# Narrow attention: two heads per stacked operand, on partitions 0 and 64, without padding

## The chip, the cores and the metric

The kernel runs on one core of one Trainium2 chip. The metric is the device time of one launch in microseconds. Before the change, three runs took 3659.43, 3660.25 and 3673.93 us; their median is 3660.25 us.

## The reference, cut to what matters

The whole program is a network of sixteen layers on an activation of 4 batch rows x 512 tokens x 128 features. Two of the sixteen are a "narrow" multi-head attention with 16 heads of 8 features each. The layers L0b and L2b compute, for each batch row,

```
q = (LN(x) Wq^T + bq) * scale      k = LN(x) Wk^T + bk      v = LN(x) Wv^T + bv
s[h] = q[h] k[h]^T                 (512 x 512 for each of 16 heads; L2b only for keys <= query)
out  = concat_h( softmax(s[h]) v[h] ) Wo^T + bo + x
```

Scale is 19.5/128 in L0b and 8^-0.5 in L2b. The other fourteen layers are not touched.

## The kernel before, in words

The activation lies transposed, features on partitions. A hardware loop runs twice, each time over two batch rows (`NB = 2`), through all sixteen layers, so each narrow attention is executed four times in all: L0b twice, L2b twice. In the profile its tiles carry the names `L0b_...` and `L2b_...`. Every engine has its own program, written out by hand (`block.sync` for the transfers, `block.tensor`, `block.scalar`, `block.gpsimd`, `block.vector`), and the engines meet only at semaphores. Nothing is scheduled by a planner: each engine takes its instructions strictly in the order of the code.

The products of q and k are made in bf16, at nearly the precision of float32. VectorE cuts q and k into three bf16 parts (`cut`, lines 1389 to 1397); the six products of parts that matter are put below each other, 8 features x 6 = 48 rows of the contraction (`Q_PART`, `K_PART`, `ROWS`). The rows are rearranged by way of a buffer in memory, `parts_dram`: `send_parts` (line 1225) writes all parts of a batch row in one transfer, and `stack` (line 1233) reads them back in twelve transfers for one **unit**. A unit is four heads of one batch row; there are `UN = 8`. Each head has a slice `qs[:, b, i, r, :]` of all 128 partitions; rows 48 to 50 of q take three bf16 parts of minus the row's maximum, against ones in k, and GpSimd has filled the other rows with zeros (q) and ones (k).

For each unit TensorE first makes all scores once with queries on the partitions (`top_scores`, line 1278, 16 of them: 4 heads x 4 blocks of 128 queries), VectorE takes the largest of each row (line 1403), the 17th step turns the 16 columns of maxima (line 1273), VectorE negates and cuts them (lines 1411 to 1421), and three small transfers put them into rows 48 to 50 of `qs` (line 1246). Then TensorE makes the scores a second time with keys on the partitions (`scores`, line 1294), with the maximum already subtracted, ScalarE takes the exponential (line 1356), and TensorE multiplies by v (`products`, line 1309), four heads side by side in 32 columns each. The v operand `vpad` carries ones in eight further columns, so the denominators come out of the same product. L2b adds a mask matmul (lines 1281 and 1297) behind each score matmul.

The order is by **slots**: 64 slots of two heads x 128 keys each. In slot s TensorE issues `scores(s)`, in even slots `products(s/2-1)`, and then two or three `top_scores` of a later unit. Before the first slot, `LEAD = 25` steps of the maxima are made. The maxima go through two PSUM banks, so TensorE can be at most two steps ahead of VectorE. After each 16 slots a finished group of eight heads is normalised: ScalarE copies the sums out, one float32 matmul spreads the denominators (line 1316), and VectorE takes the reciprocal of 128x512, multiplies and adds the bias (lines 1427 to 1431). At the end come the output projections (line 1335).

SyncE issues all transfers. Its order is: parts of batch row 0, stacks of units 0 and 1, parts of batch row 1, and then for each unit u its maxima and the stack of unit u+2.

Of the kernel before, what the change touches and what calls it, by code (L numbers as in the profile page):

```python
# [1161 lines left out]
Q_PART = (0, 0, 1, 1, 0, 2)  # L1162
K_PART = (0, 1, 0, 1, 2, 0)
# [3 lines left out]
def narrow_attention(g, name, w, causal, scale):  # L1167

    STACK = 16 * 2 * len(Q_PART)
    AHEAD = 2
    LEAD = 25
    UN = NB * 4
    with Stage(g, name) as st:  # L1180
# [12 lines left out]
        mcut = st.sb("mcut", [16, 2, 3, P], BF16)  # L1193
        inv = g.xn[:, 0, :]
        def acc(c):
            return (ln.xc, ln.sq)[c // 2][:, c % 2, :]

        proj, proj_in, cuts, cuts_act, stacked, ones_in, v_in, zero, vpad_ready = (
            st.sem(n) for n in ("proj", "proj_in", "cuts", "cuts_act", "stacked", "ones_in", "v_in", "zero", "vpad_ready"))
        top, top_in, m_steps, m_rows = (st.sem(n) for n in ("top", "top_in", "m_steps", "m_rows"))  # L1200
        score, prob, pv, inv_ready, at_ready, at_bias, out_ready, added = (
            st.sem(n) for n in ("score", "prob", "pv", "inv_ready", "at_ready", "at_bias", "out_ready", "added"))
        parted, ones_put, copied, spread = (st.sem(n) for n in ("parted", "ones_put", "copied", "spread"))
        mask_qk, mask_kq = g.cb[:, P:2 * P], g.cb[:, 2 * P:3 * P]
# [13 lines left out]
        with g.nc.Block() as block:  # L1218
            @block.sync
            def _(sp):  # L1220
                st.clear_spent(sp)

                def send_parts(b):
                    sp.wait_ge(cuts, 5 * b + 5)
                    sp.dma_start(g.parts_dram[b], cut[:, :, :, :]).then_inc(parted, 16)
                    sp.wait_ge(parted, 16 * (b + 1))

                def stack(u):
                    b, i = u // 4, u % 4
                    for j in range(len(Q_PART)):  # L1230
                        for x, part, dst in ((0, Q_PART[j], qs), (1, K_PART[j], ks)):
                            src = g.parts_dram[b, :, part, x, :].rearrange("(r i f) t -> i f r t", r=4, i=4)[i]
                            sp.dma_start(dst[DH * j:DH * j + DH, b, i, :, :], src).then_inc(stacked, 16)
                    sp.wait_ge(stacked, STACK * (u + 1))

                send_parts(0)
                sp.wait_ge(ones_in, 2)
                for u in range(AHEAD):
                    stack(u)
                send_parts(1)  # L1240
                sp.wait_ge(ones_in, 2 * NB)
                for u in range(UN):
                    b, i = u // 4, u % 4
                    sp.wait_ge(m_steps, 6 * u + 6)
                    for p in range(3):
                        sp.dma_start(qs[ROWS + p:ROWS + p + 1, b, i, :, :].rearrange("o r (t c) -> o (r t) c", c=P),
                                     mcut[:, u % 2, p, :]).then_inc(m_rows, 16)
                    sp.wait_ge(m_rows, 48 * (u + 1))
                    if u + AHEAD < UN:
                        stack(u + AHEAD)  # L1250

            @block.tensor
            def _(pe):
                ln.tensor(pe)
                for b in range(NB):
                    pe.wait_ge(ln.done, NB)
                    if b >= 1:
                        pe.wait_ge(proj_in, 2 * b)
                        pe.wait_ge(v_in, b)
                    pe.matmul(g.ps[:, 0, :], g.w(w + "_wq"), g.xn[:, b, :], start=True, stop=True)  # L1260
                    pe.matmul(g.ps[:, 1, :], g.w(w + "_wk"), g.xn[:, b, :], start=True, stop=True)
                    for t in range(KT):
                        mm = pe.matmul(g.ps[:, 2, t * P:(t + 1) * P], g.xn[:, b, t * P:(t + 1) * P], g.w(w + "_wv"), start=True, stop=True)
                    mm.then_inc(proj, 1)

                def top_scores(u, n):
# [8 lines left out]
                    if n == 0:  # L1275
                        pe.wait_ge(stacked, STACK * (u + 1))
                    r, t = n // 4, n % 4
                    mm = pe.matmul(g.ps[:, 4 + a % 2, 0:span(t)], qs[:, b, i, r, t * P:(t + 1) * P], ks[:, b, i, r, 0:span(t)],  # L1278
                                   start=True, stop=not causal)
# [4 lines left out]
                def scores(s):  # L1284

                    u, kt, half = s // 8, s // 2 % 4, s % 2
                    b, i, q0 = u // 4, u % 4, first(s // 2 % 4)
                    if kt == 0 and half == 0:
                        pe.wait_ge(m_rows, 48 * (u + 1))
                    if s >= 2:  # L1290
                        pe.wait_ge(prob, s - 1)
                    for x in range(2):
                        r, bank = 2 * half + x, 2 * (s % 2) + x
                        mm = pe.matmul(g.ps[:, bank, q0:T], ks[:, b, i, r, kt * P:(kt + 1) * P], qs[:, b, i, r, q0:T],  # L1294
                                       start=True, stop=not causal)
                        if causal:
                            mm = pe.matmul(g.ps[:, bank, q0:q0 + P], eye, mask_kq, start=False, stop=True)  # L1297
                    mm.then_inc(score, 1)

                def products(n):  # L1300

                    b, i, kt, q0 = n // 16, n // 4 % 4, n % 4, first(n % 4)
# [3 lines left out]
                    if n % 8 == 0 and b >= 1:  # L1306
                        pe.wait_ge(inv_ready, n // 8 - 1)
                    for r in range(4):
                        mm = pe.matmul(g.ps[32 * r:32 * r + 32, 6 + i // 2, q0:T], vpad[:, b, kt, 4 * r + i, :], pt[:, n % 3, r, q0:T],
                                       start=(n % 8 == 0), stop=(n % 8 == 7), skip_group_check=True)  # L1310
                    mm.then_inc(pv, 1)

                def spread_den(c):

                    pe.wait_ge(copied, c + 1)
                    pe.matmul(g.ps[:, 6 + c % 2, :], g.w("den_of"), acc(c), start=True, stop=True).then_inc(spread, 1)

                pe.wait_ge(ones_in, 2 * NB)
                pe.wait_ge(v_in, NB)
                for a in range(LEAD):  # L1320
                    top_scores(a // 17, a % 17)
                for s in range(8 * UN):
# [5 lines left out]
                    if s % 16 == 4 and s > 16:  # L1328
                        spread_den(s // 16 - 1)
                products(4 * UN - 1)  # L1330
                spread_den(2 * NB - 1)
                for b in range(NB):
                    pe.wait_ge(at_bias, 2 * b + 2)
                    for c in range(2):
                        mm = pe.matmul(g.ps[:, b, :], g.w(w + "_wo", c * P, P), acc(2 * b + c), start=(c == 0), stop=(c == 1))
                    mm.then_inc(out_ready, 1)

            @block.scalar
            def _(act):
                ln.scalar(act)  # L1340
                for b in range(NB):
                    act.wait_ge(proj, b + 1)
                    act.activation(v[:, b, :, :], g.ps[:, 2, :].rearrange("p (t c) -> p t c", c=P), ACT.Copy).then_inc(v_in, 1)
# [880 lines left out]
```

## Time and profile before

| | us |
|---|---|
| median of three runs | 3660.25 |
| the profiled execution, whole | 3659.59 |
| its span, first to last instruction | 3657.6 |
| granted TensorE clock over the span | 0.887 of full speed |
| one execution of L0b (271.7 to 469.9) | 198.2 |
| one execution of L2b (1170.0 to 1343.0) | 173.0 |

In the page's sums TensorE is busy for 75% of the span, VectorE 52%, ScalarE 40%, GpSimd 15%. These are averages over sixteen different layers. All times below are positions in the span of the profiled execution; what is said of a layer is read inside its own stretch. "PE" is TensorE's matmuls, "PEld" its weight loads, "DVE" VectorE, "ACT" ScalarE, "POOL" GpSimd, "SPq" transfers issued by SyncE. A float32 matmul shows as two PE instructions in the counts.

### The profile page before, as it was taken

To read this page: it belongs to the slowest core of one execution; us is meant where nothing else is said; L and a number is where in the kernel's file an instruction comes from. 1 tells how busy PE (TensorE), PEld (TensorE's weight loads), DVE (VectorE), ACT (ScalarE), POOL (GpSimd) and SP (SyncE) were. 2 spreads that over 40 slices of the span, in tenths; PEclk is the share of its full clock that TensorE was granted. 3 is DMA by queue.
4 is the path that set the end of the run, shared out by engine and by line. 5 is a ranking of instruction groups with operands and counts; after the bars stand their busy time and mean duration, and the time that the engine had idled before them with its cause. 6 is when DMAs were issued, how large, how long until landed. Compare 5 with 4: busy or idle time off the path is not lost. (4 is left out here: it accounts for less than half of the span.)

```text
span 3657.6 us, 33867 instructions
## 1 busy us (share of the span) xinstructions
PE 2741.8 (75%) x12082; PEld 1218.6 (33%) x12082; DVE 1890.3 (52%) x2639; ACT 1451.8 (40%) x2368; POOL 558.9 (15%) x324
## 2 busy tenths in 40 slices
PE   3565769899878579466746657789997877894677
PEld 1221145445344234123212211554443433341232
DVE  4867642455122751595649586415552237416955
ACT  2442511555234244343524424125552433443434
POOL 0533000000003101161006320000000040011600
PEclk8897977999989799799968979689999898997999
DMA  2001000000010210000000020000000102100000
GB/s 91 0 1 39 15 0 1 1 1 1 0 46 1 44 50 6 0 1 1 1 13 0 0 43 11 1 1 1 1 1 0 46 9 41 51 0 0 0 1 6
DMA packets 31504, 48.18 MB, mean 13 GB/s; under 512 B 7520, under 2 KB 19808, under 8 KB 31328
## 3 DMA queue, kind: packets, MB, share of 16 engines
q1 hardware_dynamic: 31328, 45.93, 4.8%
q8 instruction: 98, 1.61, 0.2%
q14 instruction: 78, 0.64, 0.1%
HBM read 38.18 MB, written 7.34 MB: 12 GB/s over the span
## 5 line engine op out<-in xcount | busy, mean ns | idle before, releaser
L1598 ACT ACTIVATE L1b_pr<-ps,L1b_mneg 128x512 f32<-128x512 f32 x256 | 173.8, 684 | 195.7 <-DVE L1b_mneg L1637 195.7
L518 POOL TENSOR_TENSOR xs<-xs,L2f_part 128x512 f32<-128x512 f32 x32 | 40.5, 1264 | 1287.6 <-DVE L2f_part L507 1287.6
L1356 ACT ACTIVATE L0b_pt<-ps 128x1024 f32<-128x1024 f32 x128 | 129.6, 1024 | 209.4 <-PE ps L1294 209.4
L1635 DVE TENSOR_REDUCE L1b_m<-ps 128x2 f32<-128x1024 f32 x128 | 156.7, 1224 | 105.0 <-PE ps L1502 101.0
L90 ACT ACT_TABLE_LOAD x34 | 43.6, 1283 | 419.6 <-PEq L671 181.4
L1403 DVE TENSOR_REDUCE L0b_mx<-ps 128x1 f32<-128x512 f32 x256 | 161.2, 684 | 47.7 <-PE ps L1278 45.0
L1046 POOL TENSOR_TENSOR L0a_db<-L0a_du,L0a_bs 128x1024 f32<-128x1024 f32 x64 | 150.3, 2353 | 227.8 <-ACT L0a_bs L1017 217.1
L1046 POOL TENSOR_TENSOR L3a_db<-L3a_du,L3a_bs 128x1024 f32<-128x1024 f32 x64 | 150.3, 2353 | 226.5 <-ACT L3a_bs L1017 216.0
L1356 ACT ACTIVATE L2b_pt<-ps 128x1024 f32<-128x1024 f32 (+3 forms) x128 | 88.4, 704 | 204.2 <-PE ps L1297 203.7
L1278 PE MATMUL ps<-L0b_ks,L0b_qs 128*128 128x512 bf16 x256 | 104.0, 446 | 87.0 <-DMA L0b_ks<-parts_dram 51.8
L1661 DVE COPY L1b_prt<-ps 128x512 f32<-128x512 f32 x128 | 88.5, 691 | 125.0 <-PE ps L1513 124.7
L1122 DVE TENSOR_TENSOR_SCAN L0a_hs<-ps,L0a_db 128x1024 f32<-128x1024 f32 x64 | 146.1, 2283 | 9.9 <-ACT ps L1009 8.0
L1122 DVE TENSOR_TENSOR_SCAN L3a_hs<-ps,L3a_db 128x1024 f32<-128x1024 f32 x64 | 146.1, 2282 | 9.8 <-ACT ps L1009 8.0
L1403 DVE TENSOR_REDUCE L2b_mx<-ps 128x1 f32<-128x128 f32 (+3 forms) x256 | 116.7, 486 | 54.0 <-PE ps L1281 52.4
L1502 PE MATMUL ps<-L1b_k,L1b_q 64*128 64x512 f32 x512 | 144.0, 640 | 0.0
L1525 PE MATMUL ps<-L1b_prt,L1b_v 128*64 128x512 f32 x512 | 136.7, 614 | 4.1 <-issue 2.0
L1513 PE MATMUL ps<-weights,L1b_pr 128*128 128x128 f32 x1024 | 135.8, 275 | 3.0 <-ACT L1b_pr L1598 3.0
L1278 PE MATMUL ps<-L2b_ks,L2b_qs 128*128 128x128 bf16 (+3 forms) x256 | 80.1, 347 | 76.5 <-DMA L2b_ks<-parts_dram 50.2
L1513 PEld LDWEIGHTS ps<-weights,L1b_pr 128*128 128x128 f32 x1024 | 115.6, 141 | 50.6 <-issue 43.5
L507 DVE SCALAR_TENSOR_TENSOR L2f_part<-ps,weights,L2f_masks 128x512 f32<-128x512 f32 x32 | 24.0, 751 | 205.7 <-PE ps L439 205.7
L946 PE MATMUL ps<-L0a_hc,weights 128*128 128x512 f32 x256 | 127.7, 623 | 2.7 <-DVE L0a_hc L1127 2.7
L507 DVE SCALAR_TENSOR_TENSOR L2g_part<-ps,weights,L2g_masks 128x512 f32<-128x512 f32 x32 | 24.0, 751 | 203.7 <-PE ps L439 203.7
(564 smaller groups left out, 5853.1 us busy)
## 6 DMA issues: line engine op xcount, KB each, us to landing
L2f_w<-expert_dram SPq DMA_DIRECT2D x32, 256.0 KB, 3.0
L2g_w<-expert_dram SPq DMA_DIRECT2D x32, 256.0 KB, 3.0
weights<-w_dram SPq DMA_DIRECT2D x7, 820.5 KB, 9.3
parts_dram<-L0b_cut SPq DMA_DIRECT2D x4, 768.0 KB, 3.3
L0b_qs<-parts_dram SPq DMA_DIRECT2D x96, 32.0 KB
L0b_ks<-parts_dram SPq DMA_DIRECT2D x96, 32.0 KB
parts_dram<-L2b_cut SPq DMA_DIRECT2D x4, 768.0 KB, 3.3
L2b_qs<-parts_dram SPq DMA_DIRECT2D x96, 32.0 KB
```

The source lines that it names most:

```text
L946: mm = pe.matmul(g.ps[:, k, :], g.w("ident"), hc[:, n % 2, k, :], start=(s == 0), stop=(s == NS - 1))
L1046: pool.tensor_tensor(db[:, n % 2, :, :], du[:, b, :, :], bcast(bs[:, n % 2, :], 1, 2), ALU.mult).then_inc(input_ready, 1)
L1122: dve.tensor_tensor_scan(flat(hs), decay_banks(n).rearrange("p k t -> p (k t)"), flat(db), 0.0, ALU.mult, ALU.add).then_inc(scanned, 1)
L1278: mm = pe.matmul(g.ps[:, 4 + a % 2, 0:span(t)], qs[:, b, i, r, t * P:(t + 1) * P], ks[:, b, i, r, 0:span(t)], start=True, stop=not causal)
L1356: act.activation(pt[:, n % 3, 2 * half:2 * half + 2, q0:T], g.ps[:, 2 * (s % 2):2 * (s % 2) + 2, q0:T], ACT.Exp).then_inc(prob, 1)
L1403: dve.tensor_reduce(mx[:, u, n:n + 1], g.ps[:, 4 + a % 2, 0:span(n % 4)], AX.X, ALU.max).then_inc(top_in, 1)
L1502: mm = pe.matmul(g.ps[:, 2 * (s % 2) + h, :], q[HE * h:HE * h + HE, u % 3, t * P:(t + 1) * P], k[HE * h:HE * h + HE, u % 3, :], start=True ...
L1513: mm = pe.transpose(g.ps[:, 4 + h, j * P:(j + 1) * P], pr[:, s % 2, h, j * P:(j + 1) * P], g.w("ident"))
L1525: mm = pe.matmul(g.ps[HE * h:HE * h + HE, PV, :], v[:, u % 4, j, HE * h:HE * h + HE], prt[:, u % 2, h, j, :], start=(j == 0), stop=(j == K ...
L1598: act.activation(pr[:, s % 2, h, :], g.ps[:, 2 * (s % 2) + h, :], ACT.Exp, bias=mneg[:, s % 2, h:h + 1], accum_out=total[:, u % 2, t, h:h ...
L1635: dve.tensor_reduce(m[:, s % 2, :], g.ps[:, 2 * (s % 2):2 * (s % 2) + 2, :], AX.X, ALU.max).then_inc(max_raw, 1)
L1661: dve.tensor_copy(prt[:, u % 2, 0, :, t * P:(t + 1) * P], g.ps[:, 4, :].rearrange("p (j c) -> p j c", c=P)).then_inc(turned_dve, 1)
```

## The change

Each stacked operand now holds two heads: one on partitions 0 to 47, one on partitions 64 to 111 (`HALF = 64`). `top_scores` contracts over 48 rows and `scores` over 50: the maximum goes in as two bf16 parts, not three. There is no filling of `qs` and `ks`; the ones in k come by two transfers at the start. The transfers to and from `parts_dram` have another shape and order: each part is sent by itself as soon as it is cut, q and k apart, and the parts of batch row 1 are sent after the maxima of unit 0. A stack is again twelve transfers, of 24, 16 and 8 rows. The cutting for batch row 1 and the cutting of the maxima move to GpSimd. `LEAD` is 28. The normalising is done with queries on the partitions: four transposes (`turn`), a reciprocal of 128x32 and a product of 128x256 on VectorE (`divide`), four transposes back (`turn_back`), and the copy with bias on ScalarE (`take_at`). The output of batch row 0 comes at slot 41.

The core of the diff:

```diff
-        qs = st.sb("qs", [P, NB, 4, 4, T], BF16)
-        ks = st.sb("ks", [P, NB, 4, 4, T], BF16)
-        cut = st.sb("cut", [P, 3, 2, T], BF16)
+        qs = st.sb("qs", [P, NB, H // 2, T], BF16)
+        ks = st.sb("ks", [P, NB, H // 2, T], BF16)
+        cut = st.sb("cut", [P, NB, PARTS, 2, T], BF16)
...
-                def send_parts(b):
-                    sp.wait_ge(cuts, 5 * b + 5)
-                    sp.dma_start(g.parts_dram[b], cut[:, :, :, :]).then_inc(parted, 16)
-                    sp.wait_ge(parted, 16 * (b + 1))
+                for r in range(2):
+                    sp.dma_start(ks[HALF * r + ROWS:HALF * r + ROWS + 2, :, :, :].rearrange("p b c (t k) -> p (b c t) k", k=P),
+                                 bcast(g.cb[0:2, 544:544 + P], 1, NB * H // 2 * KT)).then_inc(ones_in, 16)
+                def send(b, part):
...
+                    for x in range(2):
+                        sp.dma_start(g.parts_dram[b, part, x, :, :, :].rearrange("q c t -> c q t"), cut[:, b, part, x, :]).then_inc(sent[part], 16)
...
+                    for j, n in ((0, 3), (3, 2), (5, 1)):
+                        for r in range(2):
+                            rows = slice(HALF * r + DH * j, HALF * r + DH * (j + n))
+                            src = g.parts_dram[b, :, :, 16 * i + 8 * r:16 * i + 8 * r + 8, :, :]
+                            sp.dma_start(qs[rows, b, 2 * i:2 * i + 2, :], bcast(src[Q_PART[j], 0], 0, n)).then_inc(stacked, 16)
+                            sp.dma_start(ks[rows, b, 2 * i:2 * i + 2, :], src[K_PART[j]:K_PART[j] + n, 1]).then_inc(stacked, 16)
...
                 for u in range(UN):
+                    send_max(u)
+                    if u == 0:
+                        for part in range(PARTS):
+                            send(1, part)
                     if u + AHEAD < UN:
-                        stack(u + AHEAD)
+                        if u + AHEAD == 4:
+                            for part in range(PARTS):
+                                sp.wait_ge(sent[part], 64)
+                        load(u + AHEAD)
+                        sp.wait_ge(stacked, (u + AHEAD + 1) * LOADS)
+                    sp.wait_ge(m_rows, 64 * (u + 1))
...
                     for x in range(2):
-                        r, bank = 2 * half + x, 2 * (s % 2) + x
-                        mm = pe.matmul(g.ps[:, bank, q0:T], ks[:, b, i, r, kt * P:(kt + 1) * P], qs[:, b, i, r, q0:T],
-                                       start=True, stop=not causal)
-                        if causal:
-                            mm = pe.matmul(g.ps[:, bank, q0:q0 + P], eye, mask_kq, start=False, stop=True)
+                        r, bank = HALF * x, 2 * (s % 2) + x
+                        mm = pe.matmul(g.ps[:, bank, q0:T], ks[r:r + ROWS + 2, b, 2 * i + half, kt * P:(kt + 1) * P],
+                                       qs[r:r + ROWS + 2, b, 2 * i + half, q0:T], start=True, stop=not causal)
+                    if causal:
+                        for x in range(2):
+                            mm = pe.matmul(g.ps[:, 2 * (s % 2) + x, q0:q0 + P], eye, mask_kq, start=False, stop=True)
                     mm.then_inc(score, 1)
...
+                def turn(c):
+                    pe.wait_ge(copied, c + 1)
+                    for t in range(KT):
+                        mm = pe.transpose(g.ps[:, 6 + c % 2, t * P:(t + 1) * P], acc[:, c % 2, t * P:(t + 1) * P], g.w("ident"))
...
-                dve.reciprocal(inv, g.ps[:, 6 + c % 2, :]).then_inc(inv_ready, 1)
+                    dve.reciprocal(inv[:, :, :], rows[:, :, :, DH]).then_inc(inverse, 1)
+                    dve.tensor_tensor(att[:, :, :, 0:DH], rows[:, :, :, 0:DH], bcast(inv[:, :, :], 3, DH), ALU.mult).then_inc(scaled, 1)
...
-        g.parts_dram = nc.dram_tensor("parts_dram", [NB, P, 3, 2, T], BF16, kind="Internal").ap()
+        g.parts_dram = nc.dram_tensor("parts_dram", [NB, 3, 2, P // 2, 2, T], BF16, kind="Internal").ap()
```

Two places where instructions move. First SyncE in L0b, before the change, from the last transfers of unit 1's stack on: `parts_dram<-L0b_cut` is the sending of batch row 1, `L0b_qs<-L0b_mcut` the maxima of unit 0, and the numbers at the end are the shape that is written.

```order
L1233 DMA L0b_qs<-parts_dram 8x4x512
L1233 DMA L0b_ks<-parts_dram 8x4x512
L1225 DMA parts_dram<-L0b_cut 128x3072
L1246 DMA L0b_qs<-L0b_mcut 1x16x128 x3
L1233 DMA L0b_qs<-parts_dram 8x4x512
L1233 DMA L0b_ks<-parts_dram 8x4x512
```

The same place on SyncE with the change:

```order
L1235 DMA L0b_qs<-parts_dram 8x1024
L1236 DMA L0b_ks<-parts_dram 8x1024
L1244 DMA L0b_qs<-L0b_mcut 1x8x128 x4
L1227 DMA parts_dram<-L0b_cut 2x64x512 x6
L1235 DMA L0b_qs<-parts_dram 24x1x1024
L1236 DMA L0b_ks<-parts_dram 24x1x1024
```

Batch row 1's parts now stand between unit 0's maxima and unit 2's stack, as six transfers whose written shape has 2 as its outermost dimension; before they stood ahead of unit 0's maxima, as one of 128 rows.

Second TensorE in L2b, a slot in the steady part, before the change. `ps<-L2b_ks,L2b_qs` is a step of the maxima, `ps<-L2b_qs,L2b_ks` a head of `scores`, `ps<-cb` a mask matmul; the number at the end is partitions x columns of the result.

```order
L1278 MATMUL ps<-L2b_ks,L2b_qs 128x384
L1281 MATMUL ps<-cb 128x128
L1294 MATMUL ps<-L2b_qs,L2b_ks 128x512
L1297 MATMUL ps<-cb 128x128
L1294 MATMUL ps<-L2b_qs,L2b_ks 128x512
L1297 MATMUL ps<-cb 128x128
L1278 MATMUL ps<-L2b_ks,L2b_qs 128x512
```

A slot of the same kind with the change:

```order
L1292 MATMUL ps<-L2b_ks,L2b_qs 128x256
L1295 MATMUL ps<-cb 128x128
L1310 MATMUL ps<-L2b_qs,L2b_ks 128x512 x2
L1314 MATMUL ps<-cb 128x128 x2
L1292 MATMUL ps<-L2b_ks,L2b_qs 128x256
L1295 MATMUL ps<-cb 128x128
```

The two heads of `scores` stand together, their two masks behind them; the maxima's matmuls still have a mask behind each.

## Rows read from the trace of the kernel before

**Rows 1.** Windows: stretch, length, busy us per engine, TensorE clock, DMA share, GB/s.
```profile
271.70:469.90 198.20, 133.02 (x568) 34.97 (x568) 139.61 (x208) 72.77 (x77) 36.88 (x11) 0.86 0.12 25
1170.00:1343.00 173.00, 112.21 (x824) 50.58 (x824) 115.87 (x208) 52.15 (x77) 36.85 (x11) 0.85 0.14 29
```
**Rows 2.** Timeline of L0b's start: start, length, engine, line, operation, idle before.
```profile
287.47 6.11 DVE L1393 CAST L0b_cut<-L0b_ln_xc 128x1024 bf16<-128x1024 f32 x1
...
301.02 0.35 SPq L1225 DMA_DIRECT2D parts_dram<-L0b_cut  x1
...
304.30 0.33 SPq L1233 DMA_DIRECT2D L0b_qs<-parts_dram  x1
...
305.86 0.75 DVE L1389 CAST L0b_cut<-L0b_ln_xc 128x1024 bf16<-128x1024 f32 x1
...
311.90 1.01 PE L1278 MATMUL ps<-L0b_ks,L0b_qs 128*128 128x512 bf16 x2 [25.80 <-DMA L0b_ks<-parts_dram]
...
324.12 0.28 DVE L1411 TENSOR_SCALAR L0b_mt<-ps 16x128 f32<-16x128 f32 x1 [0.56 <-PE ps L1273]
```
**Rows 3.** The transfers, whole span: packets; issues, KB each, us to landing.
```profile
DMA packets 31504, 48.18 MB, mean 13 GB/s; under 512 B 7520, under 2 KB 19808, under 8 KB 31328
...
L2f_w<-expert_dram SPq DMA_DIRECT2D x32, 256.0 KB, 3.0
...
L0b_qs<-parts_dram SPq DMA_DIRECT2D x96, 32.0 KB
...
L0b_qs<-L0b_mcut SPq DMA_DIRECT2D x48, 4.0 KB, 1.7
```
**Rows 4.** Windows as in rows 1: the sending of parts, and one stack.
```profile
301.00:304.30 3.30, 0.00 (x0) 0.00 (x0) 0.00 (x0) 0.00 (x0) 3.30 (x1) 0.50 0.58 238
304.30:311.90 7.60, 0.00 (x1) 0.03 (x1) 6.22 (x7) 0.00 (x0) 4.53 (x7) 0.50 0.31 52
```
**Rows 5.** Timeline of VectorE in L0b, steady part.
```profile
353.53 0.28 DVE L1411 TENSOR_SCALAR L0b_mt<-ps 16x128 f32<-16x128 f32 x1 [0.45 <-PE ps L1273]
...
368.78 0.28 DVE L1411 TENSOR_SCALAR L0b_mt<-ps 16x128 f32<-16x128 f32 x1 [0.45 <-PE ps L1273]
...
371.74 3.35 DVE L1427 RECIPROCAL xn<-ps 128x512 f32<-128x512 f32 x1
...
389.66 0.28 DVE L1411 TENSOR_SCALAR L0b_mt<-ps 16x128 f32<-16x128 f32 x1 [0.45 <-PE ps L1273]
```
**Rows 6.** Timeline of L0b, all engines, one even slot.
```profile
345.12 0.59 PE L1294 MATMUL ps<-L0b_qs,L0b_ks 128*128 128x512 bf16 x2
...
345.64 1.06 PE L1309 MATMUL ps<-L0b_pt,L0b_vpad 128*32 128x512 f32 x8
...
346.64 0.61 PE L1278 MATMUL ps<-L0b_ks,L0b_qs 128*128 128x512 bf16 x2
...
347.07 3.11 DVE L1403 TENSOR_REDUCE L0b_mx<-ps 128x1 f32<-128x512 f32 x5 [1.04 <-PE ps L1278]
```
**Rows 7.** Timeline of L2b: two cuts of maxima, and masks behind matmuls.
```profile
1234.37 0.28 DVE L1411 TENSOR_SCALAR L2b_mt<-ps 16x128 f32<-16x128 f32 x1 [0.45 <-PE ps L1273]
...
1246.62 0.28 DVE L1411 TENSOR_SCALAR L2b_mt<-ps 16x128 f32<-16x128 f32 x1 [0.45 <-PE ps L1273]
...
1272.84 0.23 PE L1278 MATMUL ps<-L2b_ks,L2b_qs 128*128 128x128 bf16 x1
...
1272.90 0.22 PE L1281 MATMUL ps<-cb 128*128 128x128 bf16 x1
```
**Rows 8.** Timeline of TensorE in L1b, whose scores contract 64 rows.
```profile
762.90 1.13 PE L1488 MATMUL ps<-xn,weights 128*128 128x512 f32 x2
...
764.83 1.13 PE L1502 MATMUL ps<-L1b_k,L1b_q 64*128 64x512 f32 x4
```
**Rows 9.** Timeline of L0b's end.
```profile
457.67 1.06 PE L1309 MATMUL ps<-L0b_pt,L0b_vpad 128*32 128x512 f32 x8 [1.11 <-ACT L0b_pt L1356]
...
469.92 1.28 ACT L90 ACT_TABLE_LOAD   x1 [10.52 <-PEq L1218]
```

More of the change, by code:

```diff
@@ new lines, in send_max @@
+                def send_max(u):
+                    b, i = u // 4, u % 4
+                    for p, ready in enumerate((m_hi, m_lo)):
+                        sp.wait_ge(ready, u + 1)
+                        for r in range(2):
+                            row = HALF * r + ROWS + p
+                            sp.dma_start(qs[row:row + 1, b, 2 * i:2 * i + 2, :].rearrange("o c (t k) -> o (c t) k", k=P),
+                                         mcut[8 * r:8 * r + 8, u % 2, p, :]).then_inc(m_rows, 16)
@@ L1327, in _ @@
                         top_scores(a // 17, a % 17)
-                    if s % 16 == 4 and s > 16:
-                        spread_den(s // 16 - 1)
-                products(4 * UN - 1)
[L1331 to L1336, printed above, removed]
+                    if s % 16 == 3 and s > 16:
+                        turn(s // 16 - 1)
+                    if s % 16 == 6 and s > 16:
+                        turn_back(s // 16 - 1)
+                    if s == 41:
+                        output(0)
+                products(4 * UN - 1)
+                turn(2 * NB - 1)
+                turn_back(2 * NB - 1)
+                output(NB - 1)
             @block.scalar
@@ L1434, in _, with output @@
+                def output(b):
+                    dve.wait_ge(out_ready, b + 1)
+                    dve.scalar_tensor_tensor(out=g.xs[:, b, :], in0=g.ps[:, 7, :], scalar=g.w(w + "_bo"), in1=g.xs[:, b, :],
+                                             op0=ALU.add, op1=ALU.add).then_inc(added, 1)
+                for a in range(LEAD):
                     maxima(a // 17, a % 17)
-                for s in range(8 * UN):
+                for s in range(SLOTS):
                     for a in range(tops_before(s), tops_before(s + 1)):
@@ L1438, in _ @@
                     if s % 16 == 4 and s > 16:
[L1439 to L1444 removed]
+                        divide(s // 16 - 1)
+                    if s == 42:
+                        output(0)
+                divide(2 * NB - 1)
+                output(NB - 1)
 def wide_attention(g, name):
@@ L2086, in by_pairs @@
         out = np.zeros((4, 2, 2, 8, 2, m.shape[1]), f)
[L2087 removed]
+        out[:, :, 0] = np.asarray(m).reshape(2, 2, 4, 8, -1).transpose(2, 1, 3, 0, 4)
         return out.reshape(128, -1)
```

256 lines of the change are left out of this document (135 added, 121 removed).

## The prediction

> **What bounds the kernel now.** I read the windows first: only L0b and L2b are touched, each executed twice, 198.2 and 173.0 us a time, 742 of 3657.6 us [rows 1]. TensorE is busy for 133 of 198 us in L0b and VectorE for 140, so neither is full: what matters is how they wait for each other. Then the timeline, from the front of a layer to its end. It has four parts.
>
> The start (271.7 to 311.9): VectorE cuts q and k, and a cast takes 6.11 us (287.47) that takes 0.75 us at 305.86, with the filling over [rows 2]; GpSimd fills `qs`, `ks` and `vpad` meanwhile (36.9 us busy in the layer [rows 1]). The parts leave at 301.02, have landed at 304.30, and the first stack lets TensorE begin at 311.90: 3.3 and 7.6 us. Call 311.90 T.
>
> The lead: the search for maxima alone, VectorE-bound, 0.69 us a step (17 steps from T to 324.12, T+12.2) [rows 2].
>
> The steady part: a unit of eight slots takes 15.25 us (353.53 to 368.78) [rows 5]. In every even slot VectorE stands still for 1.04 us while TensorE makes two scores (345.12), the products (345.64) and the next step of the maxima (346.64) [rows 6]. A unit with a normalising takes 389.66 - 368.78 = 20.88 us, 5.6 more, most of it the 3.35 us reciprocal [rows 5]. In L2b a clean unit takes 12.25 us [rows 7].
>
> The end: from the last products to the next layer 469.92 - 457.67 = 12.25 us [rows 9].
>
> **The change part by part**, first for one execution of L0b.
>
> *Start: -1.* Without the filling the casts take 0.75 us each. Bias twice 0.75, three casts, two subtractions of 1.3: 6.4 us from about 280, so the last part is cut near 287 and not at 301; the first near 282. What hides this gain is the sending. The trace shows on how many of the 16 DMA engines a transfer is spread. It counts 7520 packets under 512 bytes [rows 3]. If each transfer leaves one short packet on each engine it uses, 384 stack transfers of 8 rows leave 8 each (3072), the 96 of maxima, written as 16 rows of 256 bytes, leave 16 and 16 (3072), and 86 others (64 of them the experts' weights [rows 3]) leave 16 each (1376): together 7520, exactly. With 16 for the stacks it would be 10592. So a transfer of 8 outer rows uses 8 engines, one of 128 rows 16. The new sends are written as 2 x 64 x 512: I read that as 2 engines, and since a stack keeps the mean share at 0.31, under the 0.5 of one set of 8 [rows 4], I see no rotation and take the same two each time. The Trainium skill says the same ("DMA: Bandwidth & Descriptors", the section on why a DMA increments its semaphore by 16): the largest number up to 16 that divides both sides' slowest dimension; by that the sends get 2 engines, and always the same two, the lowest ones. The trace agrees where it can (8 and 16); no row before shows 2.
>
> Six sends of 64 KB for each of two engines are 393 KB an engine. The speed of one busy engine is between 238/(0.58 x 16) = 25.6 GB/s for rows of 6 KB and 52/(0.31 x 16) = 10.5 GB/s for stacks with rows of 1 KB [rows 4]: 15 to 37 us. The sends have rows of 1 KB but go in the direction of the first row, and one engine's share lies on 64 partitions and not, with seven others, on 8; I take 19 us. 282 + 19 + 1.7 to land (a small transfer [rows 3]) = 303, against 304.3. A new stack has 4 x (8+8+1) rows of 2 KB on the busiest engine, 139 KB, 5.4 to 13.3 us; I take 6.5 + 1.7 = 8 against 7.6. So T moves by -1 us.
>
> *Lead: +1.* Three more steps at 0.69 us, less what they spare later.
>
> *The second sending: +18, and 1.5 for the slow clock after it.* The maxima of unit 0 are there at T+12.2; GpSimd cuts them (about 1 us), four small transfers about 2.4, then the sends of batch row 1 are issued by T+17.5. Their 19 us on the same two engines run to T+34.5. Behind them, on those engines, stands the stack of unit 2: T+34.5 + 6.5 + 1.7 = T+42.7. TensorE has finished 28 lead steps at T+20 and comes to unit 2's first step (step 34) in slot 3, at about T+25. It is in order, so the scores, the exponentials and the products stand too: 42.7 - 25 = 18 us, once in each execution. Before, this send stood in the lead and was covered. Later loads are in time: unit 3's stack is issued after unit 1's maxima, lands near T+53, and is wanted eight slots after the stall, T+57.
>
> *Steady part: -5.* Two heads on different halves of the array run side by side: in L1b, two matmuls of 64 rows and 512 columns take the same 1.13 us as one of 128 rows [rows 8]. So the two scores take 0.21 and not 0.43 us at 2.4 GHz, in the gap of each even slot: 0.8 us a unit, 6.4 units until the maxima are done. The five small VectorE steps that go to GpSimd lie beside the products, so they give nothing. *Normalising: -7.* Two of them fall into the part with maxima; 5.6 us becomes eight transposes at 0.25 us and 0.6 us of VectorE, partly covered: 2.3. Two times 3.3. *Output at slot 41: +2*, two float32 matmuls of 0.86 us in front of both engines. *End: -3.5*: products 1.1, copy 0.6, transposes 1.0, reciprocal and product 0.6, back 1.0, copy 0.65, output 1.9, add 0.75, and 1.1 around them: 8.7 against 12.25. Sum for L0b: -1 +1 +19.5 -5 -7 +2 -3.5 = **+6**.
>
> *L2b.* The same terms, with one more. Every step of the maxima and every pair of scores is now a matmul on half of the array's rows followed by a mask on all of them. Before, such a mask begins 0.06 us after its predecessor (1272.84, 1272.90) [rows 7]: no drain. A change of tiling is seen around the products: the scores' 2 x 0.213 us end at 345.55 and products begin at 345.64; these stream for 0.85 us but hold TensorE for 1.00 [rows 6]: 0.09 and 0.15, so 0.12 a change. The bounds are 0 and the 0.17 us by which a small matmul's 0.22 exceeds its 0.05 of streaming. The Trainium skill ("TensorEngine Tiling (Array Packing)", Key Properties) says changing the tiling mode drains the engine; the row agrees, with the sum below, and without it this term is 0. A unit has 16 steps and 8 pairs, 48 changes, of which about 42 are not covered by the wait for the last maximum: 5.0 us. The rest of a unit on TensorE is 16 x 0.2 + 8 x 0.14 + 16 x 0.06 + 4 x 0.63 + 1.2 = 9.0 us. Together 14.0 against 12.25 now: +1.8 in 6.4 units, +12 (0 to +30). The stall is again 18.5 with its slow clock, the pair saves nothing where changes are dearer. -1 +1 +18.5 +12 -7 +2 -3.5 = **+22**.
>
> Sum: 2 x (6 + 22) = +56. The profiled execution took 3659.6 us (2.0 outside the span), which is 0.7 below the median; +56 gives **3716 us**.
>
> **The rivals.**
> (a) *The sends use all 16 engines.* For: they are 128 rows in SBUF, and 7520 is an inference from a count. Against: the same count for 8 rows. Then a send takes about what 301.02 to 304.30 shows, T falls 14 us instead of 1, and there is no stall: 32.5 less in each of four executions, -130: 3586 us, faster.
> (b) *The sends' rows are slow.* At 75 ns per KB row the two sendings take 29 us each, +10 at the start and +10 in the stall, four times: +80, 3796. At the stacks' 10.5 GB/s it is 37 us and the stacks themselves, 13.3 us on an engine, reach the pace of a unit: 3850 and above. For: the only rows of 1 KB in the trace go at that rate. Against: they crowd on 8 partitions.
> (c) *Changes of tiling are free or covered.* For: VectorE, not TensorE, sets the pace in much of a unit. L2b loses its 12: 3692.
> (d) *The stall is mostly covered*: unit 0's maxima come early enough and the engines alternate between sends and stack. Then 12 of 18 go: 3716 - 48 = 3668, no measurable change. Against: one queue, issued in order.
>
> **How the numbers follow.** The forecast's own case with its range of terms, 3680 to 3750, 0.45; (c) 0.12; (b) 0.17; (a) 0.18; (d) 0.08. A measurement tells about 0.5%, 18 us, from no change. Faster: (a) and a fifth of (d), and a little for gains I sized too low: 0.21. Same: the rest of (d) and the edge of (c): 0.11. Slower: 0.68. The range for 8 in 10 goes from (a) to just above (b)'s first price: 3586 to 3810; the likeliest case's own is 3680 to 3750.
>
> **What would show it.** The gap on TensorE before unit 2's first step of the maxima, ended by the transfer of its stack: 18 us if right, none under (a), 28 under (b). The first send to the last landing: 21, 5 or 31 us. The packets under 512 bytes: each send leaves 2 and not 16 short ones. Casts of 0.75 us with the first step near 311 all the same. A clean unit of L0b at 14.4 us and of L2b at 14.0 (12.2 under (c)). The end of L0b in 8.7 us. The forecast is wrong if the first steps begin before 300, or if no wait of over 10 us stands in slot 3.

## The result, and the profile after

The changed kernel takes 3753.55 us (median of four runs, 3752.31 to 3762.55) where the kernel before takes 3659.84 on the same chip: ratio 1.0252, interval 1.0223 to 1.0282. It is slower, by 94 us; I had predicted 3716, 56 us slower. The profiled execution took 3762.55 us, its span 3760.9, which is 103.3 more than before's 3657.6.

The windows of the four executions (L0b, L0b, L2b, L2b; columns as in [rows 1]):

```profile
271.50:499.40 227.90, 158.47 (x594) 34.03 (x595) 99.22 (x159) 76.36 (x82) 23.17 (x37) 0.60 0.07 22
2156.80:2358.50 201.70, 129.09 (x593) 29.75 (x592) 97.94 (x160) 75.06 (x82) 21.98 (x37) 0.75 0.08 25
1200.50:1410.90 210.40, 159.58 (x850) 56.93 (x851) 78.08 (x159) 56.35 (x82) 23.18 (x37) 0.67 0.08 24
3058.70:3269.00 210.30, 159.65 (x850) 56.59 (x848) 78.59 (x160) 55.11 (x81) 21.91 (x37) 0.67 0.08 24
```

Against 198.2 and 173.0 us [rows 1] (the second executions of before took 197.4 and 173.2) this is +30, +4, +37 and +37 us. The number to read first is the granted clock: 0.60 to 0.75, where [rows 1] has 0.86 and 0.85. Two executions of the same L0b differ by 26 us, and their clocks by 0.15.

The start and the sending, SyncE's queue and TensorE (start, length, line; before is in [rows 2]):

```profile
281.50 10.78 SPq L1227 DMA_DIRECT2D parts_dram<-L0b_cut  x6
...
300.27 0.76 SPq L1235 DMA_DIRECT2D L0b_qs<-parts_dram  x1
...
309.76 0.61 PE L1292 MATMUL ps<-L0b_ks,L0b_qs 48*128 48x512 bf16 x2 [26.96 <-DMA L0b_ks<-parts_dram]
```

The six sends leave from 281.50 and the stack may be loaded at 300.27: 18.8 us instead of 3.3 [rows 2]. Their issue alone takes 10.78 us. T is 309.76, 2.1 us earlier than in [rows 2]. The page's count of packets, to be held against [rows 3]:

```profile
DMA packets 29058, 48.33 MB, mean 13 GB/s; under 512 B 6096, under 2 KB 12240, under 8 KB 28880
```

TensorE at the end of unit 1's maxima, and at unit 2's first step:

```profile
335.07 0.38 PE L1287 MATMUL ps<-weights,L0b_mx 128*16 128x128 f32 x1
350.47 0.58 PE L1292 MATMUL ps<-L0b_ks,L0b_qs 48*128 48x512 bf16 x1 [15.02 <-DMA L0b_ks<-parts_dram]
```

TensorE at the same step in L2b:

```profile
1279.24 0.26 PE L1292 MATMUL ps<-L2b_ks,L2b_qs 48*128 48x128 bf16 x1 [13.84 <-DMA L2b_ks<-parts_dram]
```

The standstill is there, at the place and for the reason predicted: 15.0 and 13.8 us. VectorE's units, first execution of L0b, then the second (a clean unit is 15.25 us in [rows 5]):

```profile
370.32 0.28 DVE L1469 TENSOR_SCALAR L0b_mt<-ps 16x128 f32<-16x128 f32 x1 [1.91 <-PE ps L1287]
390.09 0.28 DVE L1469 TENSOR_SCALAR L0b_mt<-ps 16x128 f32<-16x128 f32 x1 [1.91 <-PE ps L1287]
...
2250.16 0.28 DVE L1469 TENSOR_SCALAR L0b_mt<-ps 16x128 f32<-16x128 f32 x1 [0.70 <-PE ps L1287]
2256.51 2.48 DVE L1465 TENSOR_REDUCE L0b_mx<-ps 128x1 f32<-128x512 f32 x4 [0.82 <-PE ps L1292]
2263.60 0.28 DVE L1469 TENSOR_SCALAR L0b_mt<-ps 16x128 f32<-16x128 f32 x1 [0.71 <-PE ps L1287]
```

Unit 3 takes 19.8 us in one execution and 13.4 in the other, in the same program. Windows (columns as in [rows 1]) show at which clock:

```profile
350.50:451.00 100.50, 90.58 (x332) 15.89 (x333) 54.32 (x88) 41.60 (x43) 3.91 (x12) 0.50 0.07 21
2241.00:2276.00 35.00, 27.88 (x171) 6.45 (x171) 26.54 (x46) 20.68 (x23) 1.96 (x6) 1.00 0.11 32
...
1299.80:1320.30 20.50, 20.50 (x98) 6.09 (x97) 8.07 (x18) 6.12 (x9) 0.98 (x3) 0.50 0.06 20
1336.30:1351.90 15.60, 15.42 (x98) 5.54 (x97) 7.92 (x17) 6.12 (x9) 0.98 (x3) 0.80 0.09 27
```

For 100 us of the first L0b the granted clock is 0.50, which is 1.2 GHz, though TensorE is busy in 90.6 of them. In the second it is 1.00, 2.4 GHz, with TensorE busy in 27.9 of 35. So the low clock lasts long after the standstill is over, while TensorE is busy. (At half the clock the same matmul holds TensorE twice as long, so the two busy shares can't be compared as amounts of work.) The last two rows are units of L2b.

### The profile page after: what moved, and what is told of

Read it like the earlier page. It is cut to its first block and busy times, and to the rows that moved or that the text cites. A ratio compares the mean times of both kernels' runs of the same rounds, so it can differ in the third digit from the quotient of the medians.

```text
span 3760.9 us, 34111 instructions
## 1 busy us (share of the span) xinstructions
PE 2857.3 (76%) x12170; PEld 1225.7 (33%) x12178; DVE 1731.3 (46%) x2443; ACT 1461.0 (39%) x2384; POOL 504.2 (13%) x428
## 5 line engine op out<-in xcount | busy, mean ns | idle before, releaser
L1292 PE MATMUL ps<-L0b_ks,L0b_qs 48*128 48x512 bf16 x256 | 114.7, 532 | 117.0 <-DMA L0b_ks<-parts_dram 84.3
L1292 PE MATMUL ps<-L2b_ks,L2b_qs 48*128 48x128 bf16 (+3 forms) x256 | 100.4, 392 | 84.0 <-DMA L2b_ks<-parts_dram 82.0
L116 PE MATMUL ps<-xs,weights 128*128 128x512 f32 x128 | 80.0, 757 | 73.1 <-PEq L220 27.1
L946 PE MATMUL ps<-L3a_hc,weights 128*128 128x512 f32 x256 | 129.3, 629 | 2.7 <-DVE L3a_hc L1127 2.7
L946 PE MATMUL ps<-L0a_hc,weights 128*128 128x512 f32 x256 | 126.7, 618 | 2.7 <-DVE L0a_hc L1127 2.7
```

The lines of the kernel that those rows point to most:

```text
L946: mm = pe.matmul(g.ps[:, k, :], g.w("ident"), hc[:, n % 2, k, :], start=(s == 0), stop=(s == NS - 1))
L1292: mm = pe.matmul(g.ps[:, 4 + a % 2, 0:span(t)], qs[r:r + ROWS, b, 2 * i + c, t * P:(t + 1) * P], ks[r:r + ROWS, b, 2 * i + c, 0:span(t)], ...
```

## The experiments

All changes of time are against runs of the kernel before on the same chip. Three theories stood against each other for the low clock: S, the standstill brings it about; N, the matmuls that use only 48 or 50 of the array's 128 rows do; D, the changes of tiling do (the switching of the array between one matmul of 128 rows and two halves).

**1. The kernel before on fewer rows.** Its operands hold zeros times ones below row 50, so their contraction can be cut without changing a result.

```diff
-                    mm = pe.matmul(..., qs[:, b, i, r, ...], ks[:, b, i, r, ...], ...)
+                    mm = pe.matmul(..., qs[0:48, b, i, r, ...], ks[0:48, b, i, r, ...], ...)
```

(Scores 0:51; in the second kernel both are 0:72, which is over half of the array.)

> The kernel before, its maxima steps contracting rows 0 to 47 and its scores rows 0 to 50 of the same operands instead of all 128 (the other rows are zero times one); nothing else changes. Theory N and theory D: the granted clock falls to 0.50 in whole units of the steady part, where before it is 1.00; a unit of L0b at the slow clock takes 19 to 20 us instead of 15.25 and L2b's 18 to 20 instead of 12.25, so some 3700 to 3800. Theory S: the clock stays at 1.00, L0b as before; L2b is longer only by the changes of tiling, 42 x 0.12 us a unit less what is covered: 3660 to 3690.

> The kernel before, maxima steps and scores contracting rows 0 to 71 instead of all 128: over 64 rows, so the tiling of the array stays as before, but nearly half of its rows are not in use. Theory N (rows in use decide the clock): stretches at 0.50 in the steady part, 3680 to 3760. Theory D (changes of tiling) and theory S (standstill): no difference from before, 3660.

Measured: 3942.21 us, ratio 1.0767 (1.0749 to 1.0784), and 3753.68, ratio 1.0267 (1.0226 to 1.0308). Both kernels make the same matmuls of the same lengths as before. First 48 rows, a unit of L0b and one of L2b:

```profile
362.40:385.80 23.40, 22.17 (x66) 4.28 (x65) 11.85 (x22) 8.68 (x9) 0.00 (x0) 0.50 0.10 18
1291.00:1316.30 25.30, 24.42 (x98) 7.49 (x98) 9.25 (x22) 5.63 (x8) 0.00 (x0) 0.50 0.11 17
```

Every unit of all four executions runs at 0.50, and a clean one takes 23.4 us in L0b (15.25 before) and 25.3 in L2b (12.25). With 72 rows, two stretches of L0b, one in each execution:

```profile
397.80:421.10 23.30, 22.06 (x66) 4.48 (x65) 11.87 (x22) 8.67 (x9) 0.00 (x0) 0.50 0.11 18
2191.80:2222.20 30.40, 25.49 (x131) 6.36 (x130) 22.83 (x44) 16.75 (x17) 0.00 (x0) 1.00 0.17 28
```

A whole unit at 0.50 beside units at 1.00 (which take 15.25 us, as with 128 rows), without the long standstill of the changed kernel. There is a short one in front, though. In the first unit with a normalising TensorE waits for VectorE. First the kernel before, then 72 rows, the same step of the first L0b:

```profile
376.99 1.21 PE L1278 MATMUL ps<-L0b_ks,L0b_qs 128*128 128x512 bf16 x2 [2.81 <-DVE L0b_mx L1403]
382.26 1.21 PE L1278 MATMUL ps<-L0b_ks,L0b_qs 72*128 72x512 bf16 x2 [2.81 <-DVE L0b_mx L1403]
```

Windows behind it, two of the kernel before and then one of 72 rows:

```profile
377.00:383.00 6.00, 6.00 (x18) 1.26 (x18) 3.11 (x5) 2.05 (x2) 0.00 (x0) 0.50 0.22 27
385.00:389.00 4.00, 3.17 (x16) 0.77 (x16) 2.99 (x6) 2.88 (x3) 0.00 (x0) 1.00 0.00 0
...
382.30:397.80 15.50, 14.26 (x40) 3.09 (x41) 8.34 (x14) 5.12 (x5) 0.00 (x0) 0.50 0.08 10
```

The same wait of 2.8 us is followed by the low clock in both. With 128 rows it is 1.00 again about 6 us after the wait. With 72 it stays at 0.50 to the end of the unit and through the whole next one (the window 397.80:421.10); in the second L0b the next unit is wholly at 0.50 too, in L2b it is at 0.80 and 1.00. So what the rows decide here is how long the low clock lasts.

With 72 rows the tiling is never changed around these matmuls, which the masks show. L2b with 72 rows, then with 48, both at 0.50:

```profile
1295.16 0.53 PE L1278 MATMUL ps<-L2b_ks,L2b_qs 72*128 72x384 bf16 x1
1295.48 0.31 PE L1281 MATMUL ps<-cb 128*128 128x128 bf16 x1
1295.59 0.63 PE L1278 MATMUL ps<-L2b_ks,L2b_qs 72*128 72x512 bf16 x1
```

```profile
1300.69 0.50 PE L1278 MATMUL ps<-L2b_ks,L2b_qs 48*128 48x384 bf16 x1
1301.13 0.29 PE L1281 MATMUL ps<-cb 128*128 128x128 bf16 x1
1301.35 0.61 PE L1278 MATMUL ps<-L2b_ks,L2b_qs 48*128 48x512 bf16 x1
```

From start to start the 384 columns take 0.32 us with 72 rows and 0.44 with 48, the mask 0.11 and 0.22: a change of tiling costs 0.11 to 0.12 us. But the clock stays low with 72 rows too, so D alone cannot explain it. S in the form that it takes the long standstill is contradicted by both. N holds, and of the three kernels the one with more rows has more of the full clock. From 72 to 48 rows the tiling changes as well, so that step alone doesn't show what the rows do.

**2. A standstill in the kernel before.** Batch row 1's parts are sent behind unit 0's maxima, four times over.

```diff
-                send_parts(1)                       (ahead of the first maxima)
...
+                    if u == 0:
+                        send_parts(1)
```

> The kernel before (128 rows everywhere) with a standstill of TensorE where the changed kernel has its own: batch row 1's parts are sent, four times over, behind unit 0's maxima, and unit 2's stack stands behind that. Four sendings of 3.3 us and what lies around them are about 16 us, of which the lead covers 2: 12 to 15 us in front of unit 2's first step, in each of four executions, 3660 + 50 to 60 = 3715. Theory N (rows in use): the clock is back at 1.00 within 5 us of the standstill and the clean units behind it take 15.3 us in L0b and 12.0 to 12.3 in L2b, as without it. Theory S (the standstill): they stay at 0.50 and take 20 us and more, 3780 or above.

Measured: 3715.85 us, ratio 1.0156 (1.0136 to 1.0175). TensorE in L0b, then windows from the end of the standstill on:

```profile
336.47 1.07 PE L1311 MATMUL ps<-L0b_pt,L0b_vpad 128*32 128x512 f32 x8
347.92 1.01 PE L1280 MATMUL ps<-L0b_ks,L0b_qs 128*128 128x512 bf16 x2 [10.38 <-DMA L0b_ks<-parts_dram]
```

```profile
345.00:348.00 3.00, 0.08 (x1) 0.11 (x2) 0.00 (x0) 0.00 (x0) 0.00 (x0) 0.50 0.24 26
351.00:354.00 3.00, 3.00 (x13) 0.50 (x12) 0.60 (x2) 1.02 (x1) 0.00 (x0) 0.53 0.31 74
354.00:364.00 10.00, 7.78 (x39) 2.01 (x38) 7.50 (x13) 5.12 (x5) 0.00 (x0) 1.00 0.16 17
363.90:379.10 15.20, 12.59 (x65) 3.18 (x65) 11.45 (x22) 8.57 (x9) 0.00 (x0) 1.00 0.18 28
```

10.4 us of standstill (10.8 in L2b; I had expected 12 to 15). The clock falls to 0.50 in it and is 1.00 again 6 us after it; the clean units behind it run at 1.00 as in the kernel before. With 128 rows in use this standstill costs its own length and about 2 us more (unit 2 takes 27.8 us, a clean one 15.25). This was the rule by which I had priced the slow clock at 1.5 us; it is right for the kernel before and wrong for the changed one.

**3. Full rows added to the changed kernel.** A matmul of 128 rows into the bank that the next step of the maxima overwrites.

```diff
+                    pe.matmul(g.ps[:, 4 + a % 2, 0:span(t)], eye, g.cb[:, 0:span(t)], start=True, stop=True)
                     mm = pe.matmul(g.ps[:, 4 + a % 2, 0:span(t)], qs[r:r + ROWS, ...], ks[r:r + ROWS, ...], ...)
```

> The changed kernel with one more matmul ahead of each step of the maxima: all 128 rows of two constant tiles into the bank that the step then overwrites (512 columns in L0b, 128 to 512 in L2b); results are unchanged. It adds 16 x 0.21 = 3.4 us of TensorE to a unit of L0b at full clock, 6.8 at half. Theory N (the clock follows the rows in use): it holds 1.00 after the standstill, a clean unit of L0b takes 14 to 15.5 us instead of 19.8, the first execution of L0b gains 20 us and the others 0 to 5: 3710 to 3750, no slower than the changed kernel in spite of the added work. Rival theory S (it is the standstill that keeps the clock low): the units stay at 0.50 and grow to 25 us in L0b and 24 in L2b: 3850 or more.

Measured: 3818.49 us, ratio 1.0439 (1.0403 to 1.0474). Units 3 to 7 of both executions of L0b, and of L2b:

```profile
386.20:472.80 86.60, 83.97 (x419) 21.77 (x426) 56.57 (x91) 43.36 (x45) 4.92 (x15) 1.00 0.06 19
2277.10:2363.70 86.60, 83.98 (x419) 21.75 (x426) 56.55 (x90) 43.36 (x45) 4.93 (x15) 1.00 0.06 19
1311.70:1394.00 82.30, 80.72 (x578) 32.89 (x586) 41.97 (x91) 30.78 (x45) 4.92 (x15) 1.00 0.07 21
```

The clock is as theory N said from unit 3 to the end of the maxima: 1.00 in all four executions, where the changed kernel has anything from 0.50 to 1.00. These five units of L0b take 86.6 us in spite of the added work, in the first execution of the changed kernel 99.2 and in its second 80.5. Two things did not come as expected. The clock was not back right behind the standstill (8.0 us here) but only at the end of unit 2, with TensorE busy all the while:

```profile
357.60:386.20 28.60, 28.02 (x80) 4.42 (x82) 11.07 (x16) 8.20 (x8) 0.00 (x0) 0.50 0.05 15
```

And the time was wrong: the lead and unit 1, still at 0.50, got 13 us longer in L0b, and at full clock a clean unit is 16.3 and not 14 to 15.5 us. That each added matmul also brings a change of tiling is a likely reason, not one that was tested. So this supports the cause and is no remedy. The same matmuls on the kernel of experiment 4:

> The same added matmuls on the kernel with sends of 64 rows (3675 us). Theory N: units at 1.00, L0b 14 to 15.5 us a clean unit, L2b 16 to 17.5; L0b's two executions gain 20 and 5, L2b's lose or gain up to 10: 3640 to 3680. Theory S would give the same clock as without them, 0.65 to 0.85 in the four layers, and 3720 or more.

Measured: 3740.05 us, ratio 1.0224 (1.0197 to 1.0251); again 16.3 us a clean unit of L0b from unit 3 on, and again slower by the lead. The expected time was missed in the same way, and so was the clock in one place, unit 3 of the second L2b:

```profile
3112.60:3137.60 25.00, 24.28 (x112) 7.04 (x113) 8.01 (x17) 6.12 (x9) 0.98 (x3) 0.50 0.05 17
```

All other units from 3 on ran at 0.97 to 1.00. Full rows in part of the matmuls keep the clock up, but don't always bring it back within a few microseconds once it is down.

**4. The sends on all engines.** Twelve transfers of 64 rows replace six of 2 x 64.

```diff
-                        sp.dma_start(g.parts_dram[b, part, x, :, :, :].rearrange("q c t -> c q t"), cut[:, b, part, x, :])
+                        for c in range(2):
+                            sp.dma_start(g.parts_dram[b, part, x, :, c, :], cut[HALF * c:HALF * c + HALF, b, part, x, :])
```

> The changed kernel, its parts sent as twelve transfers of 64 rows in place of six of 2 x 64 rows. All theories: if a transfer of 64 outer rows uses all 16 engines, the sending takes 3 to 6 us and not 18.7, the first step of L0b comes near 296 and not at 309.8, and the 15 us standstill in front of unit 2 is gone: 29 us less in each of four executions, 3753 - 116 = 3637. Theory S (TensorE stays at 1.2 GHz because of the standstill): without it the clock rises soon after the lead, clean units of L0b take 13.4 us instead of 19.8 and those of L2b under 16 instead of 20.5: 3590 or less. Theory N (the operands of 48 and 50 rows keep the clock low) and theory D (the changes of tiling do): whole units at a granted clock of 0.50 stay, in L0b at 19.8 us, in L2b at 20: 3637 and not under 3620.

Measured: 3674.87 us, ratio 1.0041 (1.0021 to 1.0061), 79 us less than the changed kernel (77 by the two ratios). The page and L0b:

```profile
DMA packets 30498, 48.34 MB, mean 13 GB/s; under 512 B 7536, under 2 KB 13680, under 8 KB 30320
```

```profile
279.89 7.55 SPq L1228 DMA_DIRECT2D parts_dram<-L0b_cut  x12
288.99 0.80 SPq L1236 DMA_DIRECT2D L0b_qs<-parts_dram  x1
...
332.21 0.58 PE L1293 MATMUL ps<-L0b_ks,L0b_qs 48*128 48x512 bf16 x1 [7.41 <-DMA L0b_ks<-parts_dram]
```

There are 1440 more short packets than in the changed kernel, which is 96 x 16 - 48 x 2: its 48 sends used 2 engines each, if those of 64 rows use 16, as read from [rows 3]. The sending takes 9.1 us, of which 7.55 are the issue of twelve transfers; the standstill is 7.4 (6.8 in L2b) and not gone, so that step of the expectation failed. Clean units at 0.50 (19.8 us) and at 1.00 (13.4) both stand in L0b, as N says.

**5. The sends earlier**, as in 4 but issued right behind `load(1)` and ahead of unit 0's maxima.

> The changed kernel with sends of 64 rows (3675 us, standstill 7.7 us before unit 2), batch row 1's now issued right behind unit 1's stack and ahead of unit 0's maxima. If the standstill comes from the order in one queue, it goes: 7.7 us in each of four executions, 3675 - 31 = 3644; unit 0's maxima may come some us later, so up to 3655. If it comes from the stacks themselves (10 us each), it stays and the time is 3665 to 3680. The clock stays low for whole units all the same by theory N.

Measured: 3646.71 us, ratio 0.9971 (0.9949 to 0.9994). TensorE, L0b:

```profile
324.58 0.38 PE L1287 MATMUL ps<-weights,L0b_mx 128*16 128x128 f32 x1
327.18 0.58 PE L1292 MATMUL ps<-L0b_ks,L0b_qs 48*128 48x512 bf16 x1 [2.21 <-DMA L0b_ks<-parts_dram]
```

2.2 us are left, and in L2b under 0.5: the standstill came from the order in one queue.

The last sentence of the expectation failed. Units 3 to 7 of the first L0b and of the first L2b:

```profile
347.00:421.50 74.50, 60.87 (x347) 14.07 (x347) 53.30 (x91) 43.01 (x45) 4.90 (x15) 0.96 0.07 23
1228.00:1310.00 82.00, 81.38 (x507) 30.52 (x506) 41.57 (x91) 30.76 (x45) 4.89 (x15) 0.81 0.07 21
```

Behind unit 2 no unit of the four executions ran wholly at 0.50. In the profile of experiment 4, with 7 us of standstill, two did, and in that of the changed kernel, with 14 to 15 us, seven (one of them at 0.52). So with 48 and 50 rows the length of the standstill may well take part: S and N are not exclusive. This is one profiled launch of each kernel, and the mean clocks of the ten launches in experiments 4 and 5 overlap (0.847 to 0.863 and 0.852 to 0.868), so it is not shown.

**6. The kernel before with the new normalising alone**, then also with `qs` and `ks` filled as 4-byte elements, then also with GpSimd cutting the maxima into two parts.

```diff
-                        pool.memset(dst[:, b, :, :, :], float(j))
+                        pool.memset(dst[:, b, :, :, :].rearrange("p i r t -> p (i r t)").bitcast(F32), (0.0, 1.0019378662109375)[j])
```

(The float32 1.0019378662109375 has the bits of two bf16 ones.)

> The kernel before (operands of 128 rows, filled, one transfer of parts) with one part of the change alone: the new normalising by transposes and the output of batch row 0 at slot 41. My terms for it: two normalisings at 3.3 us less in each execution, the output +2, the end 3.5 less: 8 us in each of four executions, 3660 - 32 = 3628. With the 1.6 us that a normalising unit shows in the changed kernel at full clock (15.0 against 13.4) rather than 2.3, and L2b's 5.3: up to 3660 - 45 = 3615. Rival: the transposes stand in the way of scores and products on TensorE and give it back: 3655 to 3665.

> The same with the filling of qs and ks written as half as many elements of 4 bytes. A fill of 8192 elements of 2 bytes takes 7.14 us, one of 4096 elements of 4 bytes 3.94: four fills take 15 instead of 28.6 us, the slow casts of VectorE end 10 to 13 us sooner and the first step of each layer comes 8 to 12 us sooner: 32 to 48 us less than without. Rival: VectorE is slowed by the filled bytes and not by the time, so only 3 to 5 us in each execution are left, 12 to 20 in all.

> The kernel before with the new normalising and the faster filling (3588 us), and GpSimd, not VectorE, cuts the maxima, into two parts instead of three. My prediction put this at nothing. The rival reading of the trace: VectorE spends 1.6 us on these steps between two units (353.85 to 355.28), and a clean unit of the changed kernel at full clock is 1.85 us shorter than before though the pairs side by side give only 0.2 us in each of four slots: 1.0 to 1.2 us a unit, 14.1 instead of 15.3 in L0b and 11 instead of 12 in L2b, 6 units in four executions: 24 to 29 us, 3560. If my step was right, 3588.

Measured: 3623.23 us, ratio 0.9895 (0.9874 to 0.9915); 3587.94, ratio 0.9802 (0.9781 to 0.9823); 3577.92, ratio 0.9784 (0.9763 to 0.9805). All three beat both kernels. A normalising unit of L0b in the first of them:

```profile
367.40:383.20 15.80, 13.44 (x74) 4.03 (x73) 12.26 (x25) 8.65 (x9) 0.00 (x0) 1.00 0.16 26
```

15.8 us where [rows 5] has 20.9, at a clock of 1.00. Part of this gain is the clock too: the old unit ran at 0.50 from 377 to 383 (experiment 1), which I had not seen when I put most of its 5.6 us down to the reciprocal. The filling, first the costliest groups of the kernel before (busy, mean ns), then GpSimd and the last cast of the first batch row in the second kernel:

```profile
L1365 POOL MEMSET L0b_qs<- 128x8192 bf16 x4 | 28.6, 7138 | 99.2 <-POOLq L244 99.1
```

```profile
281.45 3.51 POOL L1390 MEMSET L0b_ks<- 128x4096 f32 x1
```

```profile
290.80 0.88 DVE L1424 CAST L0b_cut<-L0b_ln_xc 128x1024 bf16<-128x1024 f32 x1
```

A fill takes 3.51 us for 7.14, and the third cast 0.88 where the first of these kernels has 6.12 and [rows 2] 6.11 for the second; TensorE's first step comes 8 us sooner in each of the four executions. In the third kernel VectorE only waits where the five small steps stood (clean units of L0b again 15.3 us, of L2b 11.7 for 12.0). Its ratio cannot be told from the second's, and the 24 to 29 us of the rival reading did not come.

## Why the prediction was right in direction and 38 us short

*The start, the sending, the engines: right.* From the first send to the last landing 18.8 us for 21, then 9.5 for 8 to the first step, two engines, T 2.1 us earlier for 1. Rival (a) is out. Its price was too good: with sends on 16 engines experiment 4 has 9.1 us for a sending and a standstill of 7.4, where I had 3.3 and none.

*The standstill: right mechanism, 15 for 18 us* (14 in L2b). It began at T+25.7 and ended at T+40.7, for 25 and 42.7. Experiments 4 and 5 show its two parts, two engines and one queue in order. Rival (d) is out, and (b) too: the sends were as fast as taken.

*Steady part and normalising: right at the clock that I assumed.* At full clock the even slot's wait is 0.82 us for the 0.84 predicted, a clean unit 13.4 for 14.4, one with normalising 15.0 at a clock of 0.96: 1.6 more for the 2.3 predicted (14.6 at 1.00 in experiment 4). The full microsecond under my 14.4 is at the unit's end, where the five small steps of VectorE stood. My "they give nothing" holds in the kernel before (experiment 6), and this difference says that it does not hold once the pairs run side by side; that the one uncovers the other was not tested by itself.

*Changes of tiling: right*, 0.11 to 0.12 us for 0.12, at a clock of 0.50. (At 1.00 a mask of 128 columns in L2b takes 0.16 us from start to start in the changed kernel, and 128 columns take 0.06 in [rows 7]: 0.10.) The Trainium skill ("TensorEngine Tiling (Array Packing)", Key Properties) says that changing the mode drains the engine; experiment 1 agrees. Rival (c) is out.

*The end:* from the last products to the next layer 10.6 us (487.27 to 497.82) in the first L0b, 9.5 in the second, for 8.7. The clock was 0.57 in the first and 0.84 in the second; that the end takes 8.7 at full clock is not shown.

*What failed is one term: "1.5 for the slow clock after it".* The prediction gives no row for it. I took from the kernel before that the clock comes back a few microseconds after TensorE is busy again. Its matmuls use all 128 rows; mine would use 48 and 50. From unit 2 to unit 6 the first L0b ran at 0.50. Set against units at full clock (those of the second L0b and of experiment 4) that is 6.3 to 7.4 us in each of five units, about 33 us; the second L0b lost about 10 (one unit at 0.50, parts of two), and each L2b about 19 if a clean unit is worth the 14.0 that I predicted (no whole clean unit of it ran at 1.00; the nearest was 14.4 at 0.91, in experiment 4). Together some 80 us where the prediction had 6. Without them the profiled execution would be about 20 us slower than before and not 103, where my other terms came to 50. They were too dark, by 3 to 4 us in each standstill and by about 6 in each L0b's units: at full clock its units 2 to 7 add up to 85.4 us (four clean ones of 13.4, 14.6 and 17.1) for 101.8 before, 16.4 less where steady part, normalising and output had 10. The rest, with the 5 us outside the four executions, is not split further. Shown by runs is that fewer rows in use, with nothing else changed, make the low clock last (experiment 1, 72 rows); experiments 2 and 3 agree. That the rows alone decide is not shown: experiment 5 leaves a part to the standstill. The split of the 103 us is worked out. Outside the four executions the span is 5 us shorter than before; the cause of that was not looked for.

That the measured time lies inside the range, 3586 to 3810, is luck as far as the mechanism goes. The upper end was set for slow sends, rival (b), which did not come; the slow clock had no rival and no range. A term short by some 75 us was in part made up by others that were too dark by about 27 in sum, and even so the time lies above the likeliest case's own range, which ended at 3750.

The Trainium skill ("TensorE: Matmul & The Clock Gate", Part 1) lets the clock follow how busy TensorE has been. The traces agree that the clock falls after a wait, of 2.8 us and of 10.4. They do not bear it out as a matter of busy time alone: 90% busy at 0.50, 80% busy at 1.00, and in experiment 1 the same matmuls in the same order at 1.00 with 128 rows and at 0.50 with 48. By the measurement, how many rows each matmul uses counts too.

Still open: why the second L0b went up to 1.00 at 2241 and down again at 2278, and the first did not, in the same program. Open as well is what brings the clock back. It isn't full rows alone: the kernel before, with 128 rows, runs its lead at 0.50 too (18 us from 311.9, TensorE busy in 13.8 of them), and in experiment 3 unit 2 stayed there with TensorE always busy.

## What to carry to other kernels

Before narrowing a contraction, look at the granted clock: rows of zeros cost no time at TensorE (a unit at 1.00 takes 15.25 us with 128 rows and with 72), and taking them away left the whole steady part at half the clock here; try it first by slicing the operands of the old kernel (two lines, 3660 to 3942 us). Read a DMA's engines from its outermost dimension, and put a large send ahead of the small ones that start the next stage. And when a change with many parts loses, run its parts on the old kernel: the new normalising alone gave 1.05%, and with the filling in 4-byte elements 2.0%.

## What the runs showed of the hardware that I had not expected

- A granted clock of 0.50 for 100 us with TensorE 90% busy, when the matmuls use 48 and 50 rows; with 72 rows some units at 0.50, with 128 no whole unit in the steady part.
- A wait of TensorE of 2.8 us is followed by a clock of 0.50: for some 7 us with 128 rows, for at least 39 us with 72.
- What issuing costs depends on the transfer: the six sends on 2 engines took 10.78 us to issue, 1.8 each, twelve of half the size on 16 engines 7.55, 0.63 each. The one transfer of before, 128 rows of 6 KB, took 0.35 [rows 2]. Whether engines, rows or row length decide it, no run here separates.
- A fill goes by elements: 7.14 us for 8192 bf16 elements a partition, 3.51 for the same bytes as 4096 float32. VectorE's casts of 128x1024 take 1.6 to 6.1 us while it lasts and 0.7 to 0.9 after it.
